# A two-layer attention and expert kernel: router logits tile by tile in a reordered head, two VectorE shuffles as transfers within SBUF, the maxima's rows copied by ScalarE, and a new set of priorities

## Time and profile before

| | us |
|---|---|
| median of three runs | 1403.82 (1399.67 to 1408.38) |
| profiled execution, whole time | 1405.52 |
| profiled execution, span of the core | 1403.7 |
| TensorE busy / VectorE / ScalarE / GpSimd | 1321.2 / 1026.9 / 854.1 / 475.9 |
| mean granted TensorE clock | 0.978 of full speed |

### The profile page before, as it was taken

One profiled execution on the slowest core, in us unless ns is written; L12 is line 12 of the kernel. 1 busy time (PEld: TensorE's weight loads), 2 busy tenths in 40 slices (PEclk: granted clock), 3 DMA queues, 4 the chain that ended last, 5 costly groups with the idle time before them and its releaser, 6 DMA issues.

```text
span 1403.7 us, 25415 instructions
## 1 busy us (share of the span) xinstructions
PE 1321.2 (94%) x10009; PEld 541.6 (39%) x10009; DVE 1026.9 (73%) x1554; ACT 854.1 (61%) x1106; POOL 475.9 (34%) x445
## 2 busy tenths in 40 slices
PE   7999998989989999989999998999998999989998
PEld 6444333333334444443333333433333333333333
DVE  5534778789935348698988878798878788977727
ACT  5344347688784355256667577856668766745573
POOL 4554430010111766463244216214306144331130
PEclk7999999999999999999999999999999999999999
DMA  6523101000001711011111010111001101010100
GB/s 169 128 64 71 28 11 34 15 2 2 2 2 33 205 51 39 7 32 24 35 24 25 1 24 1 24 34 26 1 1 24 24 16 34 11 31 1 31 2 16
DMA packets 31869, 45.69 MB, mean 33 GB/s; under 512 B 5940, under 2 KB 12788, under 8 KB 31700
## 3 DMA queue, kind: packets, MB, share of 16 engines
q1 hardware_dynamic: 31752, 44.08, 13.5%
HBM read 25.39 MB, written 1.18 MB: 19 GB/s over the span
## 4 chain that ended last, share of the span: by engine, by line
PE 70%; ACT 9%; DVE 9%; issue 6%; SPq 3%; DMA 2%; POOL 1%; ACTq 0%; DVEq 0%; POOLq 0%
PE ps L1303 13%; PE ps L1406 12%; PE ps L1348 7%; ACT PR L1484 6%; PE ps L1289 5%; PE ps L1269 5%; PE ps L1271 4%; PE ps L1270 4%; PE ps L1928 3%; PE ps L1367 2%; DVE BM L1574 2%; PE ps L1417 2%; PE ps L1281 2%; PE ps L1363 1%; PE ps L1418 1%
## 5 line engine op out<-in xcount | busy, mean ns | idle before, releaser
L1484 ACT ACTIVATE PR<-ps 128x1024 f32<-128x1024 f32 x432 | 430.3, 1028 | 175.9 <-PE ps L1303 154.9
L1574 DVE TENSOR_REDUCE BM<-ps 128x2 f32<-128x1024 f32 (+2 forms) x384 | 349.9, 951 | 51.3 <-PE ps L1289 50.4
L1303 PE MATMUL ps<-QS,KS 48*128 48x512 f16 (+7 forms) x2688 | 294.8, 330 | 34.3 <-ACT PR L1484 24.6
L1406 PE MATMUL ps<-PR,VS 128*32 128x512 f32 (+3 forms) x2304 | 235.8, 502 | 5.0 <-ACT PR L1484 3.3
L1303 PEld LDWEIGHTS ps<-QS,KS 48*128 48x128 f16 (+1 forms) x2688 | 114.3, 95 | 214.4 <-ACT PR L1484 92.0
L1616 POOL TENSOR_SCALAR_AFFINE_SELECT PR<-PR 128x512 f32<-128x512 f32 x128 | 82.3, 657 | 305.6 <-ACT PR L1484 305.6
L1289 PE MATMUL ps<-KS,QS 48*128 48x128 f16 (+2 forms) x1728 | 159.9, 272 | 6.6 <-DVE BM L1574 2.7
L1567 DVE TENSOR_REDUCE BM<-ps 128x8 f32<-128x1024 f32 x96 | 116.9, 1219 | 27.1 <-PE ps L1289 26.8
L1289 PEld LDWEIGHTS ps<-KS,QS 48*128 48x128 f16 x1728 | 68.2, 94 | 122.2 <-issue 47.9
L1269 PE MATMUL ps<-YA,QS 128*128 128x512 f16 x256 | 99.6, 389 | 0.8 <-DVE RX L1533 0.7
L1270 PE MATMUL ps<-YA,QS 128*128 128x512 f16 x256 | 99.3, 388 | 0.0
(11 more groups left out here) (305 smaller groups left out, 2092.0 us busy)
## 6 DMA issues: line engine op xcount, KB each, us to landing
PR<-gates SPq DMA_DIRECT2D x32, 512.0 KB, 12.3
QS<-KS SPq DMA_DIRECT2D x64, 128.0 KB
QS<-KS SPq DMA_DIRECT2D x64, 64.0 KB
WM<-W_in SPq DMA_DIRECT2D x1, 2048.0 KB, 11.0
QS<-HL SPq DMA_DIRECT2D x48, 32.0 KB
KS<-HL SPq DMA_DIRECT2D x48, 32.0 KB
QS<-CT SPq DMA_DIRECT2D x96, 2.0 KB
PR<-x SPq DMA_DIRECT2D x4, 256.0 KB, 4.0
```

The lines of the kernel that those rows point to most:

```text
L1303: ins = pe.matmul(ps[pair][:, w, off:off + cols], KS[rows, ks, kt * P:(kt + 1) * P], QS[rows, qs, (ph + 1) * TT - cols:(ph + 1) * TT], sta ...
L1406: ins = pe.matmul(dst[32 * j:32 * j + 32, TT - cols:TT], v, PR[:, buf, j, off:off + cols], start=(g == 0), stop=(g == NGRP[ph] - 1))
L1484: act.activation(dst, src, ACT.Exp, scale=0.125 if lat else 1.0).then_inc(sig["exp"], 1)
L1574: ins = dve.tensor_reduce(BM[:, ph, p, :, qt - 4 * ph, part], bnk[:, :, off:off + nk * P], AX.X, ALU.max)
```

## The change

- **Logits.** In the head each tile's four logits matmuls are issued as soon as that tile is normalized (`pe_logits` inside `pe_load`); "rlg" keeps only the last tile. Before the second router, tiles 0 to 2 become tasks "rla" with rank 50, at the end of the first part's plan.
- **Head.** All four tiles' statistics come early on VectorE; ScalarE's steps are interleaved over tiles; 17 filler matmuls of 512 columns are put into `pe_load` (`pe_idle`); the last four heads' `pe_comp` moves there too. ScalarE's eight zero writes go from the head to just before gelus 8 to 15 of the first expert stage, with a semaphore of their own.
- **Sums.** "den" stays a shuffle in quads 3, 7, 11 and 15. In the other 18 quads it becomes "dnq": four DMAs, one for each group of 32 partitions, each copying one row of 512 floats to 32 partitions.
- **Row exchange.** "swp" becomes two DMAs on SyncE for each quad (even rows from odd ones and the reverse).
- **Copies.** "ct" (48 times) and "gtc" (8 times, the gate rows of the second expert network, L2231) go from VectorE to ScalarE.
- **Priorities.** New COST and LAND values, a longer PORT, new ORDER and (second part) WISH. All task orders and filler counts follow from these.

Left out below: the remaining lines of COST, the wiring of semaphores and counts, and the removed copies in the VectorE functions.

```diff
@@ -111,20 +111,21 @@
...
-    COST = {"turn": 0.2, "proj": 1.9, "m4": 0.2, "ct": 0.27, "crow": 1.2, "den": 0.72, "ev": 0.58, "ln": 0.63,
+    COST = {"turn": 0.2, "proj": 1.9, "m4": 0.2, "ct": 0.27, "crow": 1.2, "dnq": 2.0, "den": 0.72, "ev": 0.58, "ln": 0.63,
...
-            "scl": 0.75, "rlg": 4.6, "ro": 0.34, "rxp": 0.31, "rrk": 0.8, "rtp": 0.48, "gd": 0.4, "cmc": 0.6, "cmp": 2.0}
-    LAND = {"crow": 2.5, "put": 4.0, "egb": 2.4, "gd": 2.3, "ro": 0.0}
+            "scl": 0.75, "rlg": 1.0, "rla": 0.93, "ro": 0.34, "rxp": 0.31, "rrk": 0.8, "rtp": 0.48, "gd": 0.4, "cmc": 0.6, "cmp": 2.0}
+    LAND = {"crow": 2.5, "dnq": 3.0, "swp": 2.5, "put": 4.0, "egb": 2.4, "gd": 2.3, "ro": 0.0}
...
-    PORT = {"exl", "ewl", "scl", "gwl", "mup", "krot", "krl"}
-    ORDER = {"ACT": ("eg", "vc", "rxp", "exh", "ewh", "cmc", "ev", "qkh", "exp", "rx", "vln", "ln", "vex", "sq"),
+    PORT = {"exl", "ewl", "scl", "scb", "gwl", "wql", "mup", "krot", "krl", "rotd", "rotl", "rt", "cv", "dts", "bd",
+            "st2", "st3"}
+    ORDER = {"ACT": ("ct", "eg", "vc", "rxp", "exh", "ewh", "cmc", "ev", "qkh", "exp", "rx", "vln", "ln", "vex", "sq"),
              "DVE": ("ro", "exl", "cen", "ewl", "qkl", "eup", "add", "m4", "ct", "red", "den", "scl", "eh"),
              "POOL": ("et", "on", "vs"),
-             "SP": ("gd", "crow", "put", "egb")}
+             "SP": ("gd", "crow", "dnq", "put", "egb")}
...
-            self.take(tn, "misc", add("DVE", "ct", ("ct", n, ph), tn, ("crow", n - 1, ph) if n else None))
+            self.take(tn, "misc", add("ACT", "ct", ("ct", n, ph), tn, ("crow", n - 1, ph) if n else None))
...
-            add("ACT", "ln", ("ln", n, ph), ("den", n, ph))
+            sums = add("DVE", "den", ("den", n, ph), ("ev", n, ph)) if n % NQ == NQ - 1 else add("SP", "dnq", ("dnq", n, ph), ("ev", n, ph))
+            add("ACT", "ln", ("ln", n, ph), sums)
             add("ACT", "rx", ("rx", n, ph), ("ln", n, ph))
...
         self.router()
-        for i in range(2):
-            self.add("ACT", "cm", ("cmc", i), self.add("PE", "cm", ("cmp", i), ("rlg",)))
+        self.add("ACT", "cm", ("cmc", 0))
...
+            x = self.add("PE", "rla", ("rla", t), ("scl", 2, t), ("pv", NN - 1) + LAST_PV)
+        self.take(("rla", 0), "misc", ("scl", 2, NT - 1))
 
...
-                     "rx"),
-             "DVE": ("ro", "exl", "eh", "gtc", "scl", "den", "cen", "ct", "ewl", "scb", "hf", "krot", "m4", "rt", "eup",
-                     "cv", "dt0", "gt", "mup", "bd", "kl", "oup", "st3", "mya", "cp", "bt", "krl", "wql", "rotl", "dts",
-                     "latl", "fup", "ksw", "swp", "scn", "km", "st2", "add", "rotd", "red", "fya", "gwl"),
-             "POOL": ("mk", "pct", "on", "mk", "pbt", "rot", "ff", "xql", "et", "xl", "psg"),
-             "SP": ("wl2", "egb", "wl1", "crow", "put", "gd", "st", "kput")}
-    WISH = {"scm": 3, "unm": 2, "leadm": 3, "upm": 3, "bldm": 3, "sc": 2.04, "sc1": 1.24, "un0": 1.98, "un2":
-            2.39, "lead": 4, "un1": 1.05, "une": 1.17, "pv3": 0.82, "ahead": 3, "pv": 2.84, "qk": -1.92, "vl":
-            8.18, "proj": 9.87, "ed": 1, "mean": -0.05, "eu": 1.13, "eu1": 0.05, "mode": 0.46, "bldf": -2.69,
-            "bld2": 3.15, "bld": 2.15, "up": -0.36, "dn": 2.88, "short": -0.61}
+    ORDER = {"ACT": ("ewh", "ge", "gtc", "ev", "ct", "krh", "vex", "th", "eg", "sg", "sq", "roth", "rex", "dx", "kh",
+                     "vln", "exh", "rxp", "exp", "si", "xh", "lath", "ab", "xqh", "dl", "de", "ve0", "vc", "gwh", "wqh",
+                     "ln", "xp", "rx"),
+             "DVE": ("scl", "hf", "ewl", "cen", "ro", "mup", "scb", "eup", "krl", "den", "st3", "ct", "cv", "eh", "mya",
+                     "rt", "gtc", "wql", "m4", "exl", "gt", "dts", "krot", "kl", "dt0", "fup", "km", "ksw", "scn",
+                     "rotl", "cp", "st2", "latl", "rotd", "bd", "oup", "bt", "add", "red", "swp", "gwl", "fya"),
+             "POOL": ("xl", "pct", "mk", "on", "pbt", "rot", "psg", "mk", "xql", "et", "ff"),
+             "SP": ("egb", "kput", "dnq", "put", "wl1", "st", "wl2", "crow", "swp", "gd")}
...
 
+        def pe_idle(pe, to, n):
+
+            for _ in range(n):
+                pe.matmul(bank(to), KS[:, 0, 0:P], KS[:, 0, 0:TT], start=True, stop=True)
+
+        def pe_logits(pe, to, t):
+            for i in range(4 * t, 4 * t + 4):
+                ins = pe.matmul(bank(to)[:, i * E:(i + 1) * E], XN[:, i * P:(i + 1) * P], w_rt0[:, :], start=True, stop=True)
+            return ins
...
+            assert lg == 7
+            pe.wait_ge(s_zero, 1)
+            pe_idle(pe, 4, 5)
             pe.wait_ge(s_const, 1)
             for t in range(NT):
                 pe.wait_ge(s_x[t], 16)
...
+                    pe_idle(pe, 4, 4)
                 if t == 1:
                     pe.wait_ge(s_wc, 80)
                 if t >= 1:
                     pe_comp(pe, range(4 * t - 4, 4 * t))
+                    pe.wait_ge(s_xn, t)
+                    pe_logits(pe, lg, t - 1)
+            pe_comp(pe, range(H - 4, H)).then_inc(sig["cmp"], 1)
...
                 dve.memset(KS[:, h, :].bitcast(F32), 0.0).then_inc(s_zero, 1)
             stats(0)
-            for t in range(NT):
-                if t + 1 < NT:
-                    stats(t + 1)
+            stats(1)
+            shift(0)
+            stats(2)
+            shift(1)
+            stats(3)
+            for t in range(2, NT):
                 shift(t)
-                if t >= 1:
-                    normal(t - 1)
-                if t < NT - 1:
-                    plain(t)
-            normal(NT - 1)
-            plain(NT - 1)
+                normal(t - 2)
+                plain(t - 2)
+            normal(2)
+            normal(3)
...
-                act.wait_ge(s_rs, t + 1)
                 for i in range(4):
                     ins = act.activation(XS[:, t, i, :], XR[:, t, i, :], ACT.Identity, scale=RSTD[:, t, i:i + 1],
                                          bias=SHIFT[:, t, i:i + 1])
                 ins.then_inc(s_xc, 1)
+
+            act.preload_act_table_set(LN_EXP)
+            act.wait_ge(s_const, 1)
+            spread(0)
+            scale(0)
+            spread(1)
+            spread(2)
+            scale(1)
+            spread(3)
+            scale(2)
+            scale(3)
             act.wait_ge(s_const, N_CONST)
-            for h in range(8):
-                act.activation(QS[:, h, :].bitcast(F32).rearrange("p (a c) -> p a c", a=2),
-                               goon[:, :].unsqueeze(1).to_broadcast([P, 2, 256]), ACT.Copy, scale=0.0).then_inc(s_zero, 1)
+
+        def act_zero(act, h):
...
             if kind == "rlg":
-                for i in range(NTT):
-                    if i % 4 == 0:
-                        pe.wait_ge(s_xn, normed(lat, i // 4))
-                    ins = pe.matmul(single(plan, task)[:, i * E:(i + 1) * E], XN[:, i * P:(i + 1) * P], w_rt0[:, :],
-                                    start=True, stop=True)
-                ins.then_inc(sig["rlg"], 1)
+                pe.wait_ge(s_xn, normed(lat, NT - 1))
+                pe_logits(pe, plan.slot[task], NT - 1).then_inc(sig["rlg"], 1)
...
+                act.wait_ge(sig["turn"], c("turn", n, ph))
+                if n or lat:
+                    act.wait_ge(s_crow[ph], crow_value(lat, n - 1))
+                act.copy(CT[:, ph, :], single(plan, ("turn", n, ph))[0:16, 0:P]).then_inc(sig["ct"], 1)
             elif kind == "ln":
                 n, ph = args
-                act.wait_ge(sig["den"], c("den", n, ph))
+                if n % NQ == NQ - 1:
+                    act.wait_ge(sig["den"], c("den", n, ph))
+                else:
+                    act.wait_ge(s_sums[ph], sums_value(lat, n))
                 act.activation(RX[:, hq(ph)], RX[:, hq(ph)], ACT.Ln).then_inc(sig["ln"], 1)
             else:
...
-            elif kind == "ct":
-                n, ph = args
-                dve.wait_ge(sig["turn"], c("turn", n, ph))
-                if n or lat:
-                    dve.wait_ge(s_crow[ph], crow_value(lat, n - 1))
-                dve.tensor_copy(CT[:, ph, :], single(plan, ("turn", n, ph))[0:16, 0:P]).then_inc(sig["ct"], 1)
...
+        def sums_value(lat, n):
+            return 64 * ((NQ - 1) * (B * lat + n // NQ) + n % NQ + 1)
+
+        def sp_sums(sp, lat, c, n, ph):
+
+            sp.wait_ge(sig["ev"], c("ev", n, ph))
+            for j in range(QUAD):
+                row = 32 * j + (LAT if lat else HD0)
+                sp.dma_start(RX[32 * j:32 * j + 32, hq(ph)],
+                             OS[row:row + 1, hq(ph)].unsqueeze(1).to_broadcast([1, 32, TT])).then_inc(s_sums[ph], 16)
 
         def sp_crow(sp, lat, c, n, ph):
...
+                elif kind == "rla":
+                    t, = args
+                    pe.wait_ge(s_xn, normed(True, t))
...
+                if kind == "eg" and 8 <= args[0] < 16:
+                    act_zero(act, args[0] - 8)
...
                     sp_crow(sp, False, c, *args)
+                elif kind == "dnq":
...
```

(21 more changed lines are left out.)

80 lines of the change are left out of this document (48 added, 32 removed), and 4 rows, old and new, of the table COST.

## The result

The changed kernel takes 1520.18 us (median of four runs, 1512.88 to 1524.49), the kernel before, timed beside it, 1403.12 (1399.67 to 1408.38): a ratio of 1.082, 95% interval 1.078 to 1.086. That is slower by some 117 us; the forecast was 1382 with a range from 1354 to 1405. The profiled execution took 1512.88 us, the fastest of the four; its span is 1511.2.

A forecast was written before the change was run, and what follows sets the result against it. It took nothing as saturated, VectorE as nearest (83 to 90% busy in attention). Terms -6 - 2.7 - 5 - 12 + 1.5 + 1.5 + 1 = -21.7 us, from a 1403.8 median to 1382, range 1354 to 1405.

The forecast's parts named there:

- What SyncE takes over: Spread and exchange DMAs on SyncE's in-order queue: +1.5 us (0 to +10) for spreads, +1 (0 to +15) for exchanges.
- SyncE's queue becomes the bound: Rival: spreads ahead of "crow" delay the next quad's row; 1420 us in the middle, 1430 at worst; chance 0.11.
- The head: Start of the kernel: logits end 4.6 us earlier, gates 6 us earlier; -6 us, between +2 and -9.
- The second router: Before the second router, three of four logits tiles move before the final norm's last step: -2.7 us, bounds -2.7 and 0.
- The relief: Work taken off VectorE: -5 us in the first part's attention, -12 us in the second part (bounds 0 and -50).
- the relief is hidden: Rival: TensorE and ScalarE keep the pace, only head and second router gain; 1399 us, some 1407 with clock lost; chance 0.24.
- New priorities: Every task sequence changes, with no row to price it: taken as 0, bounds -12 and +12 us.

The follow-up runs named there:

- e3: Changed kernel, but each spread DMA copies 32 different partitions instead of one 32 times, denominators left out: 1398.16 us (0.996).
- e17: Changed kernel, but each spread reads 8 rows of its own group four times each, denominators left out: 1428.73 us (1.019).
- e18: Changed kernel, but each spread reads 2 rows 16 times each, denominators left out: 1630.76 us (1.164).
- e13: Kernel before in its exact order; shuffles of sums and 14 of 16 row exchanges move only 64 columns, denominators left out: 1391.96 us (0.993).
- e16: Kernel before with the planned cost of the shuffle of sums 0.75 instead of 0.72 us, no work changed: 1433.00 us (1.021).
- e2: Changed kernel with the landing time planned for a spread 6.0 instead of 3.0 us: 1468.09 us (1.044).
- e15: Kernel before with the planned cost of the copy of maxima 0.24 instead of 0.27 us, no work changed: 1424.86 us (1.015).
- e8: Changed kernel, but 16 partitions per group hold the sum and each spread reads these twice; result complete: 1399.39 us (0.999).
- e14: Kernel before in its exact order with an unread reduction of the same columns ahead of each shuffle on VectorE: 1421.32 us (1.013).
- e6: Kernel before with only the tile-by-tile logits, the filler matmuls and the reordered head: 1398.25 us (0.998).

## Why the prediction failed

**The step that failed** is "What SyncE takes over". I priced the issues of the spreads, 0.6 x 176 us, and what a spread does to a "crow" behind it, but not the landing of the spread itself. Where I named a landing at all, I took 2.4 us, "the nearest transfer within SBUF". That row is a copy from many partitions to many; a spread reads one partition 32 times. Its 5.8 us instead of 2.0 are the difference between 1520 and 1398, as e3 shows in the same order. The working wanted a bound from both sides for an operation that the trace didn't show, and I bounded the queue and not the operation.

**Who waits** was missed with it. I looked for the wait at "crow". It is at "ln", which the change gives a new wait (L1552), and behind "ln" on ScalarE stand the exponentials, behind those TensorE. The rival "SyncE's queue becomes the bound" (1420 to 1430) has the right engine and sign, but it decides by "ev" coming late, and puts 1.8 us on two spreads in three. In e3, with all the queueing and a fast landing, that rival costs little: SPq has 4% of the chain.

The Trainium skill has figures that would have raised the price. "SBUF — State Buffer", section "SBUF: two separate sides", says that DMAs reach SBUF by 16 ports, each serving four neighbouring partitions and the four that lie 32 above. "DMA: Bandwidth & Descriptors", section "Bandwidth", gives the 16 ports 435 GB/s together, which makes 27 each. By these pages the four spreads of a phase read two ports, 128 KB through each: an estimate of 4.8 us, against 0.6 when own rows use all 16, 1.2 for 16 rows and 2.4 for eight. The runs agree in order, each 1.2 to 2.4 us above its estimate: on the chain 7.16 us against 1.98, 2.44 and 4.25. Two rows reach the same two ports as one, so the estimate is 4.8 us again, and 8.47 were measured; the ports alone don't explain that case. The runs don't show that the port is the cause; rows that share a port but aren't repeated weren't tried. The same DMA page of the Trainium skill, section "Why a DMA increments its semaphore by 16 and not by 1", takes the number of engines from the outermost dimensions: eight for e17 and two for e18, as their packets say.

**The head: too large, and the clock misread.** The two profiled executions give 6.15 us for the gates, as forecast, but they are the latest of the old head and nearly the earliest of the new. The gates of the old head leave at 37.9 to 41.2 us in its five traces (before, e13 to e16; median 40.9), those of the new head at 34.9 to 39.5 in its fifteen (median 36.9). The extremes that overlap, of e2 and then of e15:

```profile
38.98 0.33 SPq L1678 DMA_DIRECT2D gates<-gT  x1
37.90 0.33 SPq L1628 DMA_DIRECT2D gates<-gT  x1
```

By medians that is 4.0 us and not 6. The first router step gains about 2 us (25.3 in the median against 27.4) and not 4.6. So the agreement of the one pair with -6 is partly luck.

The sum behind it took the clock as full until 15 us. The transposes say otherwise, of the changed kernel:

```profile
5.75 1.06 PE L1018 MATMUL ps<-identf,PR 128*128 128x128 f32 x4
...
7.31 0.60 PE L1018 MATMUL ps<-identf,PR 128*128 128x128 f32 x4
```

**The second router: right in kind, too large.** In e8 the stretch from the last logits' start to the gates is 12.9 us (433.92 to 446.85) instead of 14.3. That is 1.3 us, not 2.7: the last norm's tile still brings two groups of logits with it, 1.06 and 0.81 us.

**The relief: the rate held, the gain did not come.** I took a quarter to a half of VectorE's saved time. e13 gives 0.22 for relief and e14 0.51 for load. In e3 and e8 the rest of the span is 6.4 us shorter than before, against -12 plus the added terms. With the landing cured the change stands at 1399.39 us (e8), where the rival "the relief is hidden" had put it (1399), and not at 1382. The first part gained nothing: from first to second gates e8 takes 408.6 us, before 404.1, e6 403.1. The chain there (200 to 300 us, by line, e8) points to why:

```profile
by line: SPq L1861 24.4%; PE ps L1453 18.7%; PE ps L1354 7.9%; PE ps L1340 7.0%; ACT PR L1531 6.0%; issue 5.1%; DVE BM L1630 5.0%; SPq L1694 4.8%; PE ps L1728 3.6%; DMA RX<-OS 2.4%; SPq L1700 2.1%; PE ps L1361 2.0%; PE ps L1464 1.9%; PE ps 
```

SyncE's puts have 24.4% of it and spreads 4.8% more; before, puts had 16.2% of the same stretch. So even with the landing cured the term for SyncE, +1.5 with bounds 0 and +10, was too small: the first part of e8 takes 5.5 us more than that of e6, and whatever relief there was is used up on top. That is read from two kernels of different orders, so it is argued and not shown.

**New priorities: bounds too narrow.** I gave them 0 with bounds of 12 us. e15 and e16 put 24 to 32 us on a mere nudge. So the tables seem to belong to the change: with its own tables, e8 stands at 1399; with one entry taken back, at 1425 to 1431. How much of the 3 us between e8 and before is relief and how much a better or worse fit, no run here can tell.

**What stays open.** Whether the port or the partition itself serves the reads one by one. Where the other orders lose their 24 to 32 us: nothing here places it. And whether the change could win with new tables for the short landing. Of the complete kernels the fastest, e6 (1398.25) and e8 (1399.39), are 0.1 to 0.2% from before; nothing here beats it by what counts.

## What to carry to other kernels

Price a new DMA by its access pattern, not by its bytes: ask how many partitions it reads and writes, and take the landing from a row that has the same pattern, or bound it far up if there is none. Then ask which instruction waits for it in a fixed order and what stands behind that one; here 3.8 us more of landing cost 122 us. Where an order is computed from planned costs, first measure what a nudge without any work does; an effect smaller than that shows only between kernels with one order. And check a printed clock against the duration of an instruction whose time at full clock is known.

## What the runs showed of the hardware

- Spreads of 64 KB within SBUF land in 2.0 us from 32 source partitions, 2.4 from 16 read twice, and 5.8 from one read 32 times; eight of the last in a row move 36 GB/s. In the same place SyncE issues the eight in 10.05 us there and in 5.87 with own rows.
- A spread from two partitions is slower still (8.47 us on the chain against 7.16; 1944 ns for an issue against 592), with 14 packets fewer per transfer; eight partitions give 8 packets fewer. That fits two and eight DMA engines instead of 16.
- TensorE's clock was half at the start (transposes 1.06 us for four, against 0.60 later) and full from 7.15 us on in the changed kernel, with fillers, against 11.77 before. It fell to half again at 17.4 us, although TensorE had been busy without a gap since 9.2 us, and was full from 27.6 on.
